# A gated delta rule rewritten batch by batch on Trainium2

## What is computed

```
h = layernorm(x)
q, k, v = silu(conv4(h @ Wq)), silu(conv4(h @ Wk)), silu(conv4(h @ Wv))
g = -exp(A_log) * softplus(h @ Wfa @ Wfb + dt_bias);  beta = sigmoid(h @ Wb)
q = q / |q| * K ** -0.5;  k = k / |k|                        # |.| over a head's 128 channels
for t: S = S * exp(g_t); S = S + k_t (beta_t (v_t - S' k_t))';  o_t = S' q_t
o = o * rsqrt(mean(o * o) + 1e-5) * o_norm_w * sigmoid(h @ Wga @ Wgb)
x = x + o @ Wo
```

## Time and profile before

| | |
|---|---|
| median of three runs | 7230.36 us (7227.56 to 7233.61) |
| profiled execution | 7220.2 us, its span 7218.6 us |
| `low_rank` | 1996.4 to 2049.4 us of the span |
| start of `delta_heads` to the first product | 2049.4 to 2069.7 us |
| `delta_heads` from there | 2069.7 to 5811.4 us: PE busy 3228.6, VectorE 2808.9, ScalarE 1877.3, GpSimd 1230.3 us |
| mean granted clock of PE | 0.885 over the span, 0.96 in `delta_heads` |

### The profile page before, as it was taken

The page is one execution under the profiler, slowest core; times in us unless marked ns, Lnnn a source line. Parts: engine busy times, 40 slices in busy tenths (PEclk is TensorE's granted clock), DMA queues, the critical chain, the costliest instruction groups (busy, mean ns, idle before and its releaser), DMA issues. The chain is left out here.

```text
span 7218.6 us, 94429 instructions
## 1 busy us (share of the span) xinstructions
...
## 2 busy tenths in 40 slices
...
DMA packets 169443, 254.98 MB, mean 35 GB/s; under 512 B 23952, under 2 KB 91024, under 8 KB 168240
## 3 DMA queue, kind: packets, MB, share of 16 engines
...
...
## 5 line engine op out<-in xcount | busy, mean ns | idle before, releaser
L461 PE MATMUL states_y_ps<-states_hc,main_ident 128*128 128x512 f32 x512 | 463.9, 1022 | 272.6 <-DVE states_hc L418 272.4
L1541 POOL TENSOR_TENSOR delta_rule_suffix<-delta_rule_suffix,delta_rule_prefix 128x256 f32<-128x256 f32 x448 | 410.9, 917 | 709.7 <-DVE delta_rule_prefix L1744 685.9
L434 DVE TENSOR_TENSOR_SCAN states_hs<-states_decay,states_inp 128x512 f32<-128x512 f32 x256 | 497.7, 1949 | 73.9 <-POOL states_inp L406 49.1
L1862 PEld LDWEIGHTS delta_rule_level<-delta_rule_qb_second,delta_rule_k_first 128*128 128x128 f32 x3072 | 415.2, 202 | 219.8 <-issue 114.0
L1698 DVE SCALAR_TENSOR_TENSOR delta_rule_qkv<-delta_rule_raw,delta_rule_conv_w,delta_rule_qkv 128x512 f32<-128x512 f32 x576 | 433.0, 752 | 116.0 <-ACT delta_rule_qkv L1574 71.8
L2287 PE MATMUL attend_out_ps<-attend_probsT,attend_v_head 128*128 128x512 f32 x1024 | 481.5, 593 | 0.0
L406 POOL TENSOR_TENSOR states_inp<-states_du,states_bc 128x512 f32<-128x512 f32 x256 | 422.0, 1661 | 215.4 <-DVE states_hs L434 188.5
L1833 PE MATMUL delta_rule_proj<-kda_hT,delta_rule_w 128*128 128x512 f32 x1024 | 479.7, 613 | 0.0
L1862 PE MATMUL delta_rule_level<-delta_rule_qb_second,delta_rule_k_first 128*128 128x128 f32 x3072 | 442.6, 290 | 44.1 <-DVE delta_rule_QT L1749 28.7
L1532 POOL TENSOR_TENSOR delta_rule_k_first<-delta_rule_qkv,delta_rule_suffix 128x256 f32<-128x256 f32 x384 | 299.3, 779 | 633.0 <-PE delta_rule_level L1850 532.2
L2314 DVE TENSOR_REDUCE attend_top<-attend_scores 128x1 f32<-128x512 f32 x512 | 328.4, 683 | 158.8 <-DMA states_bc<-bc_dram 100.9
...
## 6 DMA issues: line engine op xcount, KB each, us to landing
states_bc<-bc_dram SPq DMA_DIRECT2D x128, 256.0 KB, 8.6
...
attend_q_stack<-parts_dram SPq DMA_DIRECT2D x256, 48.0 KB
attend_k_stack<-parts_dram SPq DMA_DIRECT2D x256, 48.0 KB
...
```

Of the source, the lines that this page charges most:

```text
L434: dve.tensor_tensor_scan(hs[:, n % NBUF, :], decay[:, n % NBUF, :], inp[:, n % NBUF, :], 0.0, ALU.mult, ALU.add).then_inc(scanned, 1)
L461: last = pe.matmul(y_ps[k % 2][:], g["ident"][:], hc[:, n % NBUF, :], start=False, stop=(n == STATE - 1))
L1541: pool.tensor_tensor(first, first, whole_second, ALU.mult).then_inc(suffix_done, 1)
L1862: last = pe.matmul(level_ps[(i + 1) % 2][:, c, :], left, qb_second[:, i % 2, c, :, :].rearrange("p j m -> p (j m)"), start=True, stop=True)
```

## The change

Units are now ordered batch by batch (heads inside), and all steps are written out, without a hardware loop. The parts:

- hT and the low-rank products go to DRAM and come back one batch at a time, in two buffers. The weights of q, k, v, decay and gate are loaded for each unit (before: for each head), also in two buffers.
- k is scaled by 1/|k| times the root of beta, so the level products of k with k carry beta and kb is not needed; v is scaled by the root of beta as it is copied out of its transpose (four activations instead of one). q is not scaled at all: the output's norm takes it up by a second product (q_share with the squares of q) that is summed before the Ln. beta's sigmoid is built from Exp and a reciprocal power.
- The raw copies of the projections are gone: VectorE's taps read PSUM.
- Second halves of q and k are made by one operation of 512 elements. First halves and suffix are VectorE's, so GpSimd has nothing in the levels; its k_state now waits for the last level's prefix.
- The gate is a Tanh and moves from slot 21 to slot 4. It is kept for two more units.
- The gated output of four heads is kept, and in slot 18 one output sum over four heads is made for one tile of tokens, with one addition into x. Four sums are left for the end.

```diff
+                for t in range(NT):
+                    for k in range(DT):
+                        last = pe.matmul(col_ps[:, t, :], hT[:, k, t * P:(t + 1) * P], wb[:, k, :],
+                                         start=(k == 0), stop=(k == DT - 1))
+                last.then_inc(col_done, 1)
...
+                act.wait_ge(col_done, 1)
+                act.activation(root_beta[:], col_ps[:], ACT.Exp, scale=-1.0).then_inc(col_exp, 1)
+                act.wait_ge(col_exp, 1)
+                act.activation(root_beta[:], root_beta[:], ACT.Ln, bias=g["ones"][:, 0:1]).then_inc(col_ln, 1)
+                act.wait_ge(col_ln, 1)
+                act.activation(root_beta[:], root_beta[:], ACT.Exp, scale=-0.5)
...
-        QB_SLOT, LEVEL_SLOT, GATE_SLOT, STATE_SLOT = 11, 12, 21, 26
+        QB_SLOT, LEVEL_SLOT, STATE_SLOT = 11, 12, 26
+        GATE_SLOT, NORM_K_SLOT = 4, 5
         CONV_SLOTS, SILU_SLOTS = (1, 2), (1, 3)
         V_PROJ_SLOT, V_OUT_SLOT, CONV_V_SLOTS = 3, 6, (7, 7, 9)
-        SILU_V_SLOT, V_BETA_SLOT, V_SLOT = 3, 4, 7
-        SQUARE_SLOT, NORM_SLOT, LN_SLOT, EXP_SLOT, GATED_SLOT, OUT_SLOT = 12, 13, 14, 14, 17, 18
...
-        def pipeline(engine, *stages):
...
-            def step(h, b, of):
+        def reach(engine, sem, value):
+            if value > 0:
+                engine.wait_ge(sem, value)
+
+        def pipeline(*stages):
+
+            for i in range(N + len(stages) - 1):
                 for s in range(SLOTS):
-                    for d in reversed(of):
-                        stages[d](s, h + (b - d) // B, (b - d) % B)
-
-            depth = len(stages)
...
+                def load_batch(b):
+                    j = b % 2
+                    reach(sp, v_projected, HEADS * (b - 1))
+                    reach(sp, proj_done, PROJ * (HEADS * (b - 1) - 1) + GATE + 1)
+                    sp.dma_start(fgT[:, j], g["fg_dram"][b]).then_inc(batch_loaded[j], 16)
+                    sp.dma_start(hT[:, j], g["hT_dram"][b]).then_inc(batch_loaded[j], 16)
...
+                load_batch(0)
+                for n in range(N + OUT_LAG):
+                    if n < N:
+                        load_unit(n)
+                    if n >= OUT_LAG:
+                        load_out(n - OUT_LAG)
+                    if n % HEADS == 2 and n // HEADS + 1 < B:
+                        load_batch(n // HEADS + 1)
...
                     elif slot == STATE_SLOT:
-                        pool.wait_ge(suffix_done, NL * (n + 1))
-                        pool.wait_ge(proj_read, PROJ * n)
-                        pool.tensor_tensor(k_state[:], k_n[p][:], suffix[:], ALU.mult).then_inc(k_state_done, 1)
-                        pool.wait_ge(prefix_done, NL * (n + 1))
...
-                        pool.wait_ge(silu_v_done, n + 1)
-                        pool.wait_ge(beta_loaded[p], 16 * (h * (B // 2) + b // 2 + 1))
...
                     if slot == 0:
                         act.wait_ge(proj_done, PROJ * n + DECAY + 1)
-                        act.activation(z[:], flat(bank(DECAY, p)), ACT.Identity, bias=head_params[:, 6:7]).then_inc(proj_read, 1)
...
+                                       scale=conv_w[slot][:, h, TAPS - 1:TAPS]).then_inc(first_tap, 1)
                     if slot in SILU_SLOTS:
                         i = SILU_SLOTS.index(slot)
                         act.wait_ge(conv_done, 2 * n + i + 1)
-                        act.activation(qkv[p][i][:], qkv[p][i][:], ACT.Silu).then_inc(silu_done, 1)
...
+                        act.wait_ge(proj_done, PROJ * n + GATE + 1)
+                        reach(act, o_ready, n - 2)
+                        act.activation(gate[n % 3][:], flat(proj_ps[1]), ACT.Tanh, scale=0.5).then_inc(bank_read[1], 1)
+                    elif slot == NORM_K_SLOT:
                         act.wait_ge(u1_done, n + 1)
                         act.activation(lnu[:], u1[:], ACT.Ln).then_inc(ln_done, 1)
-
...
+                        for c in range(CHUNKS):
+                            last = act.activation(v_rows[p][:, c, :], level_ps[1][:, c, :], ACT.Copy,
+                                                  scale=root_beta[:, b * TPB + c, h:h + 1])
+                        last.then_inc(v_copied, 1)
...
                     def second_halves(i):
 
                         s = HALVES[i]
-                        for j, src in enumerate((q_n[p], kb)):
-                            last = dve.tensor_tensor(qb_second[:, i % 2, :, j, :].rearrange("p c (n s) -> p c n s", s=s),
-                                                     by_chunk(halves(src[:], s, 1)), by_chunk(halves(prefix[:], s, 1)), ALU.mult)
-                        last.then_inc(qb_ready, 1)
-
-                    def conv_tap(i, back_by):
-                        return dve.scalar_tensor_tensor(qkv[p][i][:], raw[i][:, PAD - back_by:PAD - back_by + S],
-                                                        conv_w[i][:, h, PAD - back_by:PAD - back_by + 1], qkv[p][i][:],
+                        shape = [P, 2, S // (2 * s), s]
+                        dve.tensor_tensor(qk_second[:, i % 2, :, :].rearrange("p j (n s) -> p j n s", s=s),
+                                          qk[p][:].rearrange("p j (n two s) -> p j n two s", two=2, s=s)[:, :, :, 1, :],
+                                          halves(prefix[:], s, 1).unsqueeze(1).to_broadcast(shape), ALU.mult).then_inc(second_ready, 1)
+
+                    def first_halves(i):
+
+                        s = HALVES[i]
+                        dve.tensor_tensor(halves(k_first[:, i % 2, :], s, 0), halves(qk[p][:, 1, :], s, 0), halves(suffix[:], s, 0),
+                                          ALU.mult).then_inc(k_ready, 1)
...
-                            last = conv_tap(i, back_by)
...
+                    elif slot == NORM_K_SLOT:
+                        dve.wait_ge(proj_done, PROJ * n + K_NORM + 1)
+                        dve.wait_ge(beta_loaded[p], 16 * (n // 2 + 1))
+                        dve.scalar_tensor_tensor(k_scale[:], flat(proj_ps[0]), eps[:, 0:1], inv_beta[p][:],
+                                                 ALU.add, ALU.mult).then_inc(norm_scaled, 1)
...
-                        dve.wait_ge(inv_norm_done, 2 * n + 1)
-                        dve.tensor_tensor(k_n[p][:], k_n[p][:], inv_norm[1][:], ALU.mult)
...
+                        dve.wait_ge(silu_done, 2 * n + 1)
                         second_halves(0)
                     elif LEVEL_SLOT <= slot < LEVEL_SLOT + 2 * NL and (slot - LEVEL_SLOT) % 2 == 0:
                         i = (slot - LEVEL_SLOT) // 2
...
                         whole_first = halves(prefix[:], HALVES[i], 0)[:, :, HALVES[i] - 1:HALVES[i]].to_broadcast([P, S // (2 * HALVES[i]), HALVES[i]])
-                        dve.wait_ge(suffix_done, NL * n + i + 1)
+                        whole_second = halves(prefix[:], HALVES[i], 1)[:, :, HALVES[i] - 1:HALVES[i]].to_broadcast([P, S // (2 * HALVES[i]), HALVES[i]])
+                        if i == 0:
+                            dve.wait_ge(suffix_set, n + 1)
+                        else:
+                            dve.drain()
+                        dve.tensor_tensor(halves(suffix[:], HALVES[i], 0), halves(suffix[:], HALVES[i], 0), whole_second, ALU.mult)
+                        dve.drain()
+                        last = dve.tensor_tensor(halves(prefix[:], HALVES[i], 1), halves(prefix[:], HALVES[i], 1), whole_first, ALU.mult)
+                        if i == NL - 1:
+                            last.then_inc(prefix_done, 1)
+                        dve.drain()
                         dve.wait_ge(level_done, (NL + 1) * n + i + 1)
-                        if i == 0 and not first_steps(n):
-                            dve.wait_ge(to_state, CHUNKS * (n - 1))
-                        dve.tensor_tensor(halves(prefix[:], HALVES[i], 1), halves(prefix[:], HALVES[i], 1), whole_first, ALU.mult).then_inc(prefix_done, 1)
-                        dve.drain()
+                        if i == 0:
+                            reach(dve, to_state, CHUNKS * (n - 1))
                         if i + 1 < NL:
+                            first_halves(i + 1)
                             second_halves(i + 1)
...
+                        dve.scalar_tensor_tensor(gate[n % 3][:], gate[n % 3][:], 1.0, o_inv[:], ALU.add, ALU.mult).then_inc(o_inv_read, 1)
+                        dve.drain()
+                        reach(dve, out_done, GROUP * ((n - KEPT) // GROUP + 1))
...
+                def project(slot, n):
+                    if slot == ADD_SLOT and n >= GROUP:
+                        m = n - GROUP
+                        xr = g["x"][:, m // HEADS * TPB + m % GROUP, :]
+                        dve.wait_ge(out_done, m + 1)
+                        dve.tensor_tensor(xr, xr, out_ps, ALU.add).then_inc(out_added, 1)
...
+                        pe.wait_ge(bank_read[1], 3 * n + 1)
+                        pe.matmul(flat(proj_ps[1]), w_fg[p][:, 1, :], fgT[:, b % 2, 1, :], start=True, stop=True).then_inc(proj_done, 1)
```

(22 more changed lines are left out.)

481 lines of the change are left out of this document (224 added, 257 removed).

## The result

The changed kernel took 7497.5 us (median of 4 runs, 7493.3 to 7500.7), the kernel before 7231.9 us (4 runs beside them, 7227.6 to 7233.6). The ratio is 1.0369, 95% interval 1.0357 to 1.0381: slower, by more than forecast (7400), and inside the range. The profiled execution's span is 7497.5 us against 7218.6, 278.9 more.

A forecast was written before the change was run, and what follows sets the result against it. No engine fills a unit, so interlocking in-order queues bound it. Stretches 42.7 + 16.0 = 58.7, clock 1.0: 59.7 us; 63 x (59.7 - 57.5) + 31 = 170 on 7230.4: 7400 us, range 7160 to 7540.

The forecast's parts named there:

- second stretch: From product R2T in slot 17 to the next k_state transposes: 16.0 us instead of 13.2, +2.8.
- level step: One level's operations on VectorE, now including suffix and k_first: 2.62 us.
- VectorE's wait before X: After level 3, VectorE waits 1.95 us for W of slot 19, which stands behind the output sum on PE.
- First stretch: From the k_state transposes to product R2T in slot 17: 42.7 us, from 44.3 before.
- The shorter key chain: Key's chain before PE's product, without kb and with changed norm and gate steps: 1.0 us shorter.
- two predicated copies 0.66: Within a VectorE level step, two predicated copies cost 0.66 us; beside a GpSimd product one took 0.72 instead of 0.42.
- The clock: PE drops to 1.2 GHz behind pauses, 1.7 us a fall: 1.0 us added to 58.7, making 59.7 a unit.
- both places fall and the predicated copies stay slow: Rival: clock falls at both PE pauses, finest levels' copies slow by 0.3 us each: 62 us, total 7545; chance 0.12.
- Ends: Outside the units: low-rank block's small products +16 us, first product's wait 0, last output sums +15; together +31 us.
- (c): Rival: VectorE's level step stays at 2.28 us and the clock holds: 56.3 us a unit, total 7185; chance 0.30.
- (a): Rival: PE stays at 2.4 GHz in the new pauses: 58.7 us a unit, total 7337 us; chance 0.17.
- The extra load for Tanh: On ScalarE, the gate's Tanh may need its own 1.28 us table load, costing 0 to 0.6 us; taken as 0.

The follow-up runs named there:

- Experiment 6: Kernel before, head loop written out, with suffix and first halves moved to VectorE and k_state behind the last prefix: 7466.5 us.
- experiment 9: Changed kernel plus four 512-column TensorE products a unit that nobody reads, three in slot 23 and one in slot 25: 7437.2 us.
- Experiment 8: Changed kernel with output sum spread over slots 18 to 24, suffix and first halves on GpSimd, root beta's columns from 16 transposes: 6971.3 us.
- experiment 4: Kernel before with only its head loop written out: 7207.4 us, ratio 0.9975.
- experiment 3: Changed kernel with the output sum spread over slots 18 to 24 and suffix and first halves back on GpSimd: 6994.0 us.

## Why the prediction was right, and where it was short

**The sign and the main mechanism held.** Two things named as the loss of the second stretch, the four-fold sum in slot 18 and the level products on VectorE with k_state behind them, were undone one by one and together: 167, 325 and 503 us. Without them nothing of the loss is left. Experiment 6 put one of them into the kernel before and made it 259 us slower.

**Second stretch: 16.0 us forecast, 16.26 measured** without a fall. The loss in it was larger than the +2.8 of the prediction, though, because the 13.2 us that it started from held a fall: without one the stretch went from 12.2 to 16.26, +4.1. Its terms: level step 2.62 forecast, 2.78 measured (3905.86 to 3908.64), because the operation behind the second predicated copy starts 0.51 us after it (3908.13, 3908.64), not 0.33; VectorE's wait before X 1.95 forecast, 1.75 measured; k_state's wait right (3909.65 to 3910.92).

**First stretch: 42.7 forecast, 43.0 measured** in the units of experiment 9 that have no fall. That this is so near is luck. The prediction took 1.6 us off 44.3, and 44.3 held a fall of 1.1 us; without falls the stretch went from 43.2 to 43.0, 0.2 us less. The shorter key chain came: PE's pause fell from 2.42 to 1.10 us, and in fall-free units the product behind it starts 22.8 us after the transposes instead of 23.5, 0.7 earlier (1.0 forecast). That gain is still there at the product of level 2 (36.6 us behind the transposes instead of 37.3) and shrinks to 0.2 by R2T: PE waits 1.22 us for VectorE's addition into X there, where it had waited 0.80. So the level steps of this stretch did not get shorter as forecast. What failed is the term "two predicated copies 0.66". I had read 0.72 us for such a copy as GpSimd's doing, since a GpSimd product stood beside it. In the changed kernel GpSimd is idle there and the copies take 0.72 and 0.78 us, which is some 0.6 us in each of the two finest levels, and 0.3 of it arrived in the stretch. The time goes with the form: halves of 1 and 2 elements take that long, halves of 4 and more 0.42 to 0.45, before and after, with a GpSimd product beside them or none. What GpSimd did slow was the product beside it that has two SBUF inputs, the key's (840 against 418 ns). The cause exists; I had put it on the wrong instruction.

**The clock: +1.0 us forecast on top of 58.7, +1.9 measured on top of 59.3** (2.2 in the steady units). This is the step that made most of the 94 us between 59.7 and 61.2. The size of the term was wrong, and not by the number of falls: between the first and last diagonal copy there are 78 before and 86 after. All but one last 3.4 us before, but 62 of the 86 last 6.8 us, so the time at half speed went from 4.6 to 8.6 us a unit. The part of a long fall in the pause ahead of the transposes costs nothing (the second stretch is 16.26 us with and without it); the rest runs into the gapless projections and costs 1.2 to 1.9 us. A fall at the start of the second stretch costs 1.7, in 19 of 57 units. The price of 1.7 us is right for the changed kernel; in the kernel before a fall costs 1.0 to 1.1.

The prediction's words "58.7 us, with PE at full speed" also hide that its base, 57.5 us, was not at full speed: without falls the two kernels take 55.4 and 59.3 us a unit. These 3.9 us are as much as the whole rise of the mean period in the steady part (57.67 to 61.52): what falls and loop turns together added before, 2.2 us, the falls alone add after. So the loss is in the order of the work; what the clock takes has risen by no more than the loop's turns cost before.

The forecast's rival "both places fall and the predicated copies stay slow" is close to what happened, with both places falling in a third of the units; I had put it at 0.12 and 62 us because it "needs all of them". It came out at 61.2, nearer to that rival than to my 59.7.

**Ends: +31 forecast, 23.0 + 25.6 = +49 measured.** Of the first, 5.5 us are there before the low-rank block's first product (2005.9 instead of 2000.4); in the ten runs of the experiments it starts anywhere from 2002.6 to 2008.4, so they can't be called the change's. Then 17.5 us belong to the change, against 16 + 0. They came another way: the small products took 23.6 us, not at most 18, since PE ran them at a granted clock of 0.59, and the wait behind them is 20.34 us and no longer 23.96, with the loads of the weights as its end and not the masks. Experiment 8 gives these 23 us back. At the end a sum with its add takes 4.50 us (6082.78 to 6087.28), not 4.39, and the first of the five sums takes 6.64 us, most of it at half speed, so the sums add 18.2 us against 15. Another 9.9 us come between the last diagonal copy and the first of these sums, and the layers behind them take 2.5 us less.

**The sum.** 63 x (61.19 - 59.7) = 94 us and 49 - 31 = 18 us; the forecast stood on the median, and the profiled executions are 13 us further apart than the medians. 7400 + 94 + 18 - 13 = 7499.

**The rivals.** (c), a level step so cheap that the change wins, is out: 2.78 us. (a), no falls, did not come; its price would have been the 59.3 us of the fall-free units in experiment 9, 0.6 above its 58.7. The extra load for Tanh did not come: over 50 units the gate has no load in front of it, while Silu, and the Ln and the Exp behind it, have one each. The groups of the middle of the stage (busy us, mean ns | idle time before them):

```profile
L1559 ACT ACT_TABLE_LOAD x51 | 65.4, 1283 | 0.9
L1573 ACT ACT_TABLE_LOAD x50 | 64.2, 1283 | 0.9
L1578 ACT ACT_TABLE_LOAD x50 | 64.2, 1283 | 0.9
...
L1570 ACT ACTIVATE delta_rule_gate<-delta_rule_proj 128x512 f32<-128x512 f32 x50 | 29.9, 597 | 57.8 <-PE delta_rule_proj L1825 57.8
```

By the table sets of the Trainium skill ("ScalarE: Activation LUTs", Table sets), as I read them in the prediction, Tanh behind Silu would have had one; this trace does not agree. The section's table names no set for Silu, so it is the reading that fails. Between 2500 and 5500 us the straight stream has no idle time of PE above 0.3 us that no semaphore explains, where the kernel before has 13 like the 2.59 us of the earlier trace rows, and there the trace agrees with the Trainium skill ("Runtime: NRT & Kernel Launch", Instruction fetch mechanics); by experiment 4 leaving out the turns is worth 16 us and not the 50 that they seem to cost.

**Still open.** Why a filled pause moves the fall to another place instead of removing it, and why the changed kernel's falls last twice as long. In experiment 3 there are only 4 falls between the first and the last diagonal copy, and in 9 there are 45, with pauses before R2T and before X that look alike; I did not separate them.
